# Seeded tie-breaking in the list scheduler of an attention and ternary-FFN kernel

## The reference, cut to what matters

```python
xn = layernorm(x)                                  # x: 1 x 2048 x 256
q, k, v = xn @ Wq, xn @ Wk, xn @ Wv                # 8 query heads, 2 key/value heads of 32
q, k = rope(q), rope(k)
std = softmax(causal(q @ k.T / sqrt(32))) @ v
geo = softmax(causal((q[..., :3] . dir) * (k[..., :3] . dir))) @ v     # rank-1 scores
att = (std + head_scale * (geo - std)) @ Wo
z   = xn @ ternary(W_syn).T + b_syn                # 2048 x 1024
hid = where(z >= 102nd largest of its row, relu(z), 0)
ffn = layernorm(xn + hid @ ternary(W_out).T + b_out) * gamma + beta
out = x + att + ffn
```

## Time and profile before

| | us |
|---|---|
| runs | 736.84, 738.36, 742.61 (median 738.36) |
| the profiled execution | 732.19 |
| its span | 730.3 |

### The profile page before, as it was taken

How to read it: one execution, slowest core, us unless ns; L and a number is a source line. 1 busy time by engine, 2 the same in 40 slices (tenths; PEclk the granted TensorE clock), 3 DMA queues, 4 the chain that set the end, 5 groups by cost and what they waited for, 6 DMA issues and landing times. The chain is left out here.

```text
span 730.3 us, 12339 instructions
## 1 busy us (share of the span) xinstructions
PE 672.8 (92%) x4424; PEld 317.3 (43%) x4424; DVE 497.2 (68%) x976; ACT 448.9 (61%) x732; POOL 238.3 (33%) x312
## 2 busy tenths in 40 slices
PE   4689898999899999998999999999899899997997
PEld 2443443434444443443434444454444455554443
DVE  7857996585768766778776776865675586766612
ACT  5435446455765444298744534789888879985553
POOL 5523445113213120232100121333443342346723
PEclk9979998999999999999999999999999899999999
DMA  8577000002700000053000000000001000000000
GB/s 241 191 190 195 11 9 1 30 2 92 189 9 2 1 1 1 3 153 63 1 5 1 1 1 1 19 29 22 23 23 31 22 22 23 16 23 9 1 1 30
DMA packets 26194, 30.81 MB, mean 42 GB/s; under 512 B 7105, under 2 KB 21313, under 8 KB 25746
## 3 DMA queue, kind: packets, MB, share of 16 engines
q1 hardware_dynamic: 24210, 29.45, 14.3%
q10 hardware_dynamic: 1920, 0.54, 0.3%
HBM read 17.72 MB, written 11.53 MB: 40 GB/s over the span
## 5 line engine op out<-in xcount | busy, mean ns | idle before, releaser
L935 ACT ACTIVATE probs<-scores 128x1024 f32<-128x1024 f32 (+3 forms) x320 | 270.9, 893 | 226.1 <-PE acc L1481 184.9
L1172 DVE TENSOR_REDUCE piece_max<-side 128x1 f32<-128x512 f32 x190 | 126.1, 685 | 61.3 <-PE side L1371 59.1
L1474 PE MATMUL acc<-probs,v_nat 128*32 128x512 f32 (+3 forms) x1280 | 151.9, 547 | 6.8 <-POOL probs L779 5.6
L1481 PE MATMUL acc<-probs,ones_all 128*32 128x512 f32 (+3 forms) x1280 | 152.0, 547 | 0.0
L1371 PE MATMUL side<-k_stack,q_stack 128*128 128x512 f32 (+3 forms) x316 | 120.9, 432 | 10.7 <-DVE piece_max L1172 3.2
L779 POOL TENSOR_SCALAR_AFFINE_SELECT probs<-probs 128x256 f32<-128x256 f32 x128 | 54.6, 436 | 226.3 <-ACT probs L935 225.0
L1371 PEld LDWEIGHTS side<-k_stack,q_stack 128*128 128x128 f32 x316 | 54.3, 188 | 101.3 <-DVE piece_max L1172 40.2
L1456 PE MATMUL scores<-q_stack,k_stack 128*128 128x512 f32 (+3 forms) x320 | 90.9, 387 | 5.3 <-ACT probs L935 4.9
L1175 DVE CUSTOM_DVE_ANT_0 side<-side,tail_mask 128x256 f32<-128x256 f32 (+3 forms) x126 | 61.8, 498 | 19.9 <-PE side L1371 19.2
L1474 PEld LDWEIGHTS acc<-probs,v_nat 128*32 128x32 f32 x1280 | 35.8, 111 | 78.8 <-issue 59.8
L1456 PEld LDWEIGHTS scores<-q_stack,k_stack 128*128 128x128 f32 x320 | 52.9, 190 | 36.9 <-ACT probs L935 29.8
(11 more groups left out here) (170 smaller groups left out, 899.5 us busy)
## 6 DMA issues: line engine op xcount, KB each, us to landing
q_stack<-q_parked SPq DMA_DIRECT2D x12, 512.0 KB, 7.1
q_parked<-turned SPq DMA_DIRECT2D x8, 512.0 KB, 3.3
res<-in_L_attn_x_dram SPq DMA_DIRECT2D x4, 512.0 KB, 6.4
x_parked<-xn SPq DMA_DIRECT2D x4, 512.0 KB, 2.9
xT_parked<-xnT SPq DMA_DIRECT2D x4, 512.0 KB, 2.8
xz<-xT_parked SPq DMA_DIRECT2D x16, 128.0 KB, 2.5
xb<-x_parked SPq DMA_DIRECT2D x16, 128.0 KB, 2.2
out_dram<-res SPq DMA_DIRECT2D x16, 128.0 KB, 1.7
```

The source lines that it names most:

```text
L935: nc.scalar.activation(probs[:, slot % 2, pair, :, off:], scores[:, pair, :, off:], ACT.Exp, scale=ATT_SCALE if kind == 0 else 1.0).then_i ...
L1172: free(nc.vector.tensor_reduce(piece_max[:, h, p:p + 1], pt, AX.X, ALU.max), ("S",) + a)
L1474: nc.tensor.matmul(acc[D * h:D * h + D, 0, off:], v_nat[:, j, g], probs[:, slot_no[a] % 2, h // 2, h % 2, off:], start=(j == 0), stop=(j = ...
L1481: last = nc.tensor.matmul(acc[D * h:D * h + D, 1, off:], ones[:, 0:D], probs[:, slot_no[a] % 2, h // 2, h % 2, off:], start=(j == 0), stop ...
```

## The change

The planner's virtual time is cut into stretches of 25 us (`STRETCH`), and each stretch has a seed. Where the seed is 0 the scheduler decides as before. Where it is not (18 of 29 stretches; those from 200 to 350 us are all 0) a pseudo-random number sets how near in time a piece must be to compete (0.4 to 1.6 times `SLACK`), and adds 0 to 2.5 to the rank of each stream, another number for each stream and decision. Work, durations, waits and buffers are as before; only the order in the queues changes, and with it the bank numbers and the semaphore counts.

```diff
+STRETCH = 25000
+SEEDS = (2, 0, 26, 34, 44, 0, 47, 38, 0, 0, 0, 0, 0, 0, 41, 33, 40, 38, 6, 42, 48, 1025, 0, 27, 0, 8, 0, 1035, 3)
...
+    stretch, state = -1, 0
...
         first = min(b[0] for b in best)
-        close = [b for b in best if b[0] <= first + SLACK and b[3] == min(best)[3]]
-        start, rank, key, eng, flow, ns, m = min(close, key=lambda b: (b[1], b[0]))
+        n = int(first // STRETCH)
+        seed = SEEDS[n] if n < len(SEEDS) else 0
+        if n != stretch:
+            stretch, state = n, seed * 7919 + n
+        state = (state * 1103515245 + 12345) % 2147483648
+        near = SLACK * (0.4 + 1.2 * state / 2147483648) if seed else SLACK
+        close = [b for b in best if b[0] <= first + near and b[3] == min(best)[3]]
+        start, rank, key, eng, flow, ns, m = min(close, key=lambda b: (b[1] + (2.5 * ((state >> 8) * (1 + sum(map(ord, b[4]))) % 1009) / 1009 if seed else 0), b[0]))
```

## The result

| | before | after |
|---|---|---|
| median of the runs beside each other | 737.60 us (4 runs) | 719.61 us (4 runs, 718.36 to 722.44) |
| the profiled execution | 732.19 | 720.07 |
| its span, mean granted clock | 730.3, 0.974 | 718.3, 0.974 |

The ratio is 0.9757, with a 95% interval from 0.9717 to 0.9797. The two profiled executions are only 12.1 us apart: the one of before was 5 to 6 us quicker than its kernel's median, the one of after was typical. That difference is about a third of the 18 us, and most of what the forecast missed.

What follows compares the result with a forecast made beforehand. PE, busy 92% of the span, was taken as the bound. Terms -3.1 - 8.7 + 2.0 = -9.8 us gave 722.4 us against the profiled execution, 728.6 us against the median; range 721 to 739 us.

Steps and rivals of the forecast that it cites:

- The base of the sum: Profiled execution of before, 732.19 us, from which terms were subtracted; its 6.2 us gap to the median 738.36 was added back.
- The array changes: PE's queue, whole run: 501 changes of array use become 474, saving 3.1 us on the path.
- The three stalls: At 107, 573 and 656 us PE waits for cuts behind long POOL blocks; two of three granted as gone, -8.7 us.
- The first place: Stretch 107 to 122.5 us: PE's `val` waits for cuts behind POOL's mix; idle time plus half-clock loss priced 5.6 us.
- The two late ones: Stretches 573 to 587.5 and 656 to 665.2 us: PE waits for cuts behind `y_out`, priced 5.4 and 3.9 us.
- The new stall: Chunk 3, geometric, g = 0: a `y_out` now stands between the cuts of key tiles 12 and 13, +2.0 us.
- The two moves at 0: `w_cut` and transposes earlier in chunk 0, 8 `S` tiles later in chunk 1: costed at 0, at most 5.5 us.
- the clock losses move instead of going: Half-speed time behind the three stalls only shifts elsewhere: -5.1 us, 733.3 us, chance 0.22.
- The waits come back elsewhere: Each stall is replaced by another of its size, leaving only the array saving: -3.1 us, 735.3 us, chance 0.10.
- ACT as the bound: FFN work moves late, where ACT is busiest (500 to 650 us, above 95%): +8.5 us, 746.9 us, chance 0.08.
- All three stalls and no new one: All three PE waits for cuts vanish and the added `y_out` costs nothing: -16.2 us, 722.2 us, chance 0.05.
- The check I named: PE's busy time at full clock should fall by about 3 us, else the prediction is wrong from the start.

Runs made afterwards that it cites:

- the other experiment: Kernel before with `sum` drawn next to `val` over two `S` tiles, 17 array changes fewer: 742.31 us, ratio 1.0016.
- the second part: Before's order up to 191 us of the plan, the change's order from there: 729.35 us (0.9872), timed again 726.93 us (0.9847).
- the first part: The change's order up to 191 us of the plan, before's order from there: 740.37 us, ratio 1.0032; cut at 308 us instead: 738.42 us, 1.001.
- the other profile of before: Kernel before, unchanged, timed against itself and profiled again: median 738.96 us, ratio 1.0011; the profiled execution took 743.35 us.

## Why the prediction was wrong

**The base of the sum** failed, and with it the largest part of the miss. I took the profiled execution of before as it stood (37.5 us at half speed) and let its gap of 6.2 us to the median carry over to the changed kernel. The gap was not a constant of the measurement: that execution had 18.8 us less at half speed than before has on average (56.3), which at 0.34 is 6.4 us. The changed kernel runs at 35.7 us on average, so its profile and its median agree (720.07 and 719.61). Against the profiled pair the forecast of -9.8 stands beside -12.1 measured; against the medians beside -18.

**The array changes** (-3.1): right in sum, perhaps with some luck. The 116 added changes cost 0.115 us each, and 27 fewer make 3.1 us. But the prediction's prices gave 19 us for those 116 (17.5 with its share of 0.92), and 13.4 were measured (8.4 to 18.3). So the changes to columns and to full may have been priced a third too high, and the five to rows, taken at nothing, would then have made up for it. The durations in the chain are unchanged. The 17 fewer of the other experiment showed none of their 2 us; its interval leaves room for it. Where they lie: 22 of the 27 in the second part.

**The three stalls** (-8.7 as two of three): the size is not far off, since half-speed loss and idle time of the second part fell by 6.6 + 3.7 = 10.3 us. The way is wrong. The first place brings nothing (1.0032 [0.9998, 1.0065] and 1.001 [0.9976, 1.0044]): PE still waits 0.90 us there for a cut, that of another key tile, and the half-speed stretch shrank from 6.8 to 3.4 us. Nor was the late cut its cause by itself, as I had read it: with the mix moved by hand the cut was on time and the clock fell as before. The two late ones do not go by moving the blocks behind the cuts, which is how I had explained them: 0 and 3.2 us were measured. What I had named as the next late thing, the exponents, did come, with 1.20 us, and the search behind it with 1.36. In the change both places are better than by hand, presumably since everything around them is in another order too: from 565 to 600 and from 650 to 665 us PE has no wait over 0.9 us, where the hand-moved kernels have waits of 1.2 to 1.9, and there is no fall of the clock from 345 us on. With the stalls put back by force the change loses 14.6 us, more than the 9.3 that I had valued the second and third at, because those waits are 4.3 to 4.6 us, not 2.

**The new stall** (+2.0): did not come. Its `y_out` runs from 513.36 to 518.5 us, and the `val` behind it starts at 519.32 after a wait of 0.26 us; PE's longer wait just ahead, 0.68 us, is for an exponent. The alternative that I gave, the exponents being late anyway, held, and PE had other work.

**The two moves at 0**: the first part of the run shows no cost of theirs, 315.6 against 316.7 us.

**The rivals.** That the clock losses move instead of going was right for one execution of each kernel (37.5 and 37.6 us) and wrong over many (56.3 to 35.7); even in the one pair the places of the falls say little, as the other profile of before has early falls like those of the change. Its -5.1 us was further off than the forecast. The waits come back elsewhere: true of the hand-moved cuts, not of the change. ACT as the bound fell: ACT does have 137.9 of 150 us (92%) where it had 87%, but PE idles for 4% there and waits less for exponents, 3.9 us in 9 waits. All three stalls and no new one (722.2) came nearest, with a chance of 0.05; its sum of -16.2 happens to be near -18, by terms that the experiments do not bear out.

**The check I named**, PE's busy time in terms of full clock falling by about 3 us: it fell by 8.2 us (6.8 by the page, and 1.4 that more loss at half speed hides, 16.4 to 17.8). The 5 us beyond the array changes should have told of a term that the sum lacked. Nor is it all explained: about 2 us of the second part's gain, and why the changed kernel spends less time at half speed than the kernel with only its second part (35.7 to 50.6 us, and 6.8 us of time in one comparison), stay open. Extended to no half-speed time those two kernels lie within 4 us of each other (704.7 and 707.4 against 708.2 and 707.0), so most of the difference goes with the clock, but nothing run here shows what in the first part sets it.

## What to carry to other kernels

Before a sum is made against one profiled execution, compare its granted clock with those of several timed runs: here the same program took 732 to 747 us, and the clock went with it, and the gap between profile and median came with that execution's clock and did not carry over to the changed kernel. A long block ahead of short work in one queue cost, where it was put in here, what it made PE wait, plus half of the half-speed time behind it; but take the next late things from the trace before crediting its removal, since in this dense schedule such moves alone gained 0 to 3 us of a priced 9 to 13. Where a scheduler's own count ranks orders as the chip does (check with a few orders drawn blindly), searching it further can be worth more than repairing single waits: here 24.6 us against 0 to 3.

## What the runs showed of the hardware

- Executions of one unchanged kernel spread over 14 us (733.33 to 747.26), and the granted clock goes with it: 0.34 us of span for each us at 1.2 GHz.
- The places where the recorded clock falls are of two kinds. Those in the last third recur at the same work in every execution profiled with the old order there: 528, 579 and 661 us before; 539, 590 and 672 in the execution that ran 11 us later; 533, 585 and 666 with the new first part. Those in the first 350 us, where PE often waits for transfers and maxima (2.4 us for one transfer, 4.3 for maxima in before), differ between executions of the same program: before has five there in one profile and ten in the other, and that part took 313.1 us in one and 320.0 in the other.
- 8.9 us of forced waiting in two places brought back two falls in a stretch that had none. Taking a wait of 0.76 us for a cut away at the first place took none away.
- A change between the array's uses costs 0.115 us of the kernel's time on average (0.07 to 0.16 by the interval of one experiment), and shows as 0.13 us on eight matmuls in columns and 0.20 to 0.37 on four with the full array.
